# A stack of four conditioned blocks on one core: who writes the masked copies of the transposed keys in the two 16-head attention stages

## What is computed

```python
h = modulate(rmsnorm(x, norm1_w), sh_msa, sc_msa)
q, k, v = split(h @ qkv_w.T)                # 16 heads of 16
q, k = rmsnorm(q, q_norm_w), rmsnorm(k, k_norm_w)
q, k = rope3d(q, k, positions)
attn = softmax(einsum('bnhd,bmhd->bhnm', q, k) * 16 ** -0.5)
o = einsum('bhnm,bmhd->bnhd', attn, v) @ proj_w.T + proj_b
x = x + g_msa * o
```

## Time and profile before

| what | us |
| --- | --- |
| median of the runs (lowest, highest) | 2176.62 (2170.26, 2176.9) |
| the profiled execution | 2174.85 |
| its span (first to last instruction) | 2173.0 |
| PE, DVE, ACT, POOL busy in the span | 1923.1, 1320.1, 998.8, 817.1 |
| stage 1 without its ends (879 to 1190) | 311 |
| stage 2 without its ends (1510 to 1725) | 215 |

### The profile page before, as it was taken

One profiled execution on the slowest core, in us unless ns is written; L12 is line 12 of the kernel. 1 busy time (PEld: TensorE's weight loads), 2 busy tenths in 40 slices (PEclk: granted clock), 3 DMA queues, 4 the chain that ended last, 5 costly groups with the idle time before them and its releaser, 6 DMA issues. The chain is left out here.

```text
span 2173.0 us, 44682 instructions
## 1 busy us (share of the span) xinstructions
PE 1923.1 (89%) x17318; PEld 1488.1 (68%) x17318; DVE 1320.1 (61%) x2026; ACT 998.8 (46%) x1693; POOL 817.1 (38%) x733
## 2 busy tenths in 40 slices
PE   5999999999979997678887899969999889988897
PEld 3678777877867775466666677747676667776674
DVE  3454555455545554688878566757888745544554
ACT  2434433443346664456656333324555556653232
POOL 1210211021113434667777233456777633340000
PEclk7999999999999999899989999999999999999998
DMA  5100000000020000000000000010000000003222
GB/s 178 69 2 2 2 2 2 2 2 2 2 64 1 0 0 18 27 2 3 2 1 2 27 0 0 0 40 2 2 0 2 1 30 0 0 1 117 76 68 78
DMA packets 25884, 44.97 MB, mean 21 GB/s; under 512 B 3952, under 2 KB 11952, under 8 KB 25584
## 3 DMA queue, kind: packets, MB, share of 16 engines
q1 hardware_dynamic: 25712, 42.48, 5.9%
HBM read 36.18 MB, written 6.29 MB: 20 GB/s over the span
## 5 line engine op out<-in xcount | busy, mean ns | idle before, releaser
L1165 DVE TENSOR_TENSOR Glb<-Gfb,Ghb 128x512 fp32r<-128x512 f32 x176 | 164.3, 943 | 101.3 <-ACT Ghb L1116 99.6
L321 POOL TENSOR_TENSOR Tm<-Dv,MOD 128x512 f32<-128x512 f32 x96 | 110.5, 1171 | 248.7 <-DVE Dv L378 159.9
L439 PE MATMUL bank<-HH,W1b 128*128 128x512 f32 x448 | 185.0, 413 | 13.6 <-PEq L1445 7.3
L439 PE MATMUL O<-Ghb,W2b 128*128 128x512 f32 x352 | 144.1, 409 | 49.5 <-DVE Glb L1165 47.8
L440 PE MATMUL bank<-HL,W1b 128*128 128x512 f32 x448 | 178.0, 397 | 0.0
L441 PE MATMUL bank<-HH,W1b 128*128 128x512 f32 x448 | 177.9, 397 | 0.0
L459 POOL TENSOR_TENSOR spare<-RT 128x1 f32<-128x1 f32 x32 | 6.5, 202 | 414.9 <-DVE RT L450 414.9
L310 POOL TENSOR_TENSOR XS<-Tm 128x512 f32<-128x512 f32 x48 | 68.0, 1416 | 221.2 <-ACT Tm L276 221.1
L441 PE MATMUL O<-Ghb,W2b 128*128 128x512 f32 x352 | 138.6, 394 | 0.0
L440 PE MATMUL O<-Glb,W2b 128*128 128x512 f32 x352 | 138.3, 393 | 0.0
L1596 ACT ACTIVATE PTa<-bank 128x512 f32<-128x512 f32 x128 | 69.8, 594 | 126.2 <-PE bank L1476 126.1
(11 more groups left out here) (255 smaller groups left out, 5215.0 us busy)
## 6 DMA issues: line engine op xcount, KB each, us to landing
w<-l_w_dram SPq DMA_DIRECT2D x33, 256.0 KB, 3.5
wm<-w_mods_dram SPq DMA_DIRECT2D x6, 768.0 KB, 6.1
X<-xT_dram SPq DMA_DIRECT2D x16, 256.0 KB, 6.7
out_dram<-XO SPq DMA_DIRECT2D x8, 512.0 KB, 2.7
W2b_f<-l_w_dram SPq DMA_DIRECT2D x11, 256.0 KB, 5.2
WQK_f<-l_wqk_dram SPq DMA_DIRECT2D x8, 256.0 KB, 8.8
W1b_0f<-l_w_dram SPq DMA_DIRECT2D x8, 256.0 KB, 3.6
WV<-l_wv_dram SPq DMA_DIRECT2D x1, 1024.0 KB, 10.5
```

The costliest lines, as they stand in the source:

```text
L321: nc.gpsimd.tensor_tensor(Tm[:, k].rearrange("p (b t) -> p b t", t=T), Dv[:, k].rearrange("p (b t) -> p b t", t=T), m, ALU.mult).then_inc( ...
L439: nc.tensor.matmul(out, w_lo_ap, x_hi, start=first, stop=False)
L1165: nc.vector.tensor_tensor(Gl[m % gb][:], gf, Gh[m % gb][:].bitcast(F32), ALU.subtract).then_inc(g_lo.h, 1)
```

## The change

All four masked copies are written by ACT, each by one instruction of the kind of L1582; the last one counts `ka_sb`. The DVE instruction, its function and its semaphore's waits are gone. Nothing else moves.

```diff
@@ pe: weights_t
-  pe.wait_ge(ka_sb.h, ka_sb.at(tt + 2)); pe.wait_ge(kd_sb.h, kd_sb.at(tt + 2))
+  pe.wait_ge(ka_sb.h, ka_sb.at(tt + 2))
@@ pe: step, before the scores
-  pe.wait_ge(ka_sb.h, ka_sb.at(tt + 1)); pe.wait_ge(kd_sb.h, kd_sb.at(tt + 1))
+  pe.wait_ge(ka_sb.h, ka_sb.at(tt + 1))
@@ act: q_t
-  nc.scalar.activation(kb[:, :, 2], src, ACT.Copy, scale=hmask4[:, 2:3])
-  nc.scalar.activation(kb[:, :, 3], src, ACT.Copy, scale=hmask4[:, 3:4]).then_inc(ka_sb.h, 1)
+  for h in range(4):
+      last = nc.scalar.activation(kb[:, :, h], src, ACT.Copy, scale=hmask4[:, h:h + 1])
+  last.then_inc(ka_sb.h, 1)
@@ dve
-  def spread_k(tt, t):
-      dve.wait_ge(ka_sb.h, ka_sb.at(tt + 1))
-      dve.wait_ge(s_ready.h, s_ready.at(tt - 1))
-      src = TR_T4[:, 2 * P:4 * P].rearrange("p (gb k) -> p gb k", k=T)
-      nc.vector.tensor_tensor(KB[t % 2][:].rearrange("p g b h k -> p (g b) h k")[:, :, 0:2], src.unsqueeze(2).to_broadcast([P, 4, 2, T]),
-                              hmask4[:, 0:2].unsqueeze(1).unsqueeze(3).to_broadcast([P, 4, 2, T]), ALU.mult).then_inc(kd_sb.h, 1)
@@ dve: step
-  if ahead(t, more, tail, 1):
-      spread_k(tt + 1, (t + 1) % TL)
@@ dve: lead-in
-  spread_k(0, 0)
@@ end of stage
-  ka_sb.passed(NT); kd_sb.passed(NT)
+  ka_sb.passed(NT)
```

## The result

The changed kernel took 2191.64 us (median of 7 runs, 2183.33 to 2192.87) beside 2175.24 us (7 runs, 2162.93 to 2176.9) for the kernel before on the same chip: ratio 1.0075, 95% interval 1.0058 to 1.0093, so +16.4 us. The forecast was 2189.5 (+14.6), within 2180 to 2199. The profiled execution took 2192.87 us around a span of 2191.1.

A forecast was written before the change was run, and what follows sets the result against it. It took as bound the uncovered chain behind ScalarE's root at t = 3, once a chunk, and TensorE in other steps. Terms 9.9 + 2.9 + 0.7 + 1.4 - 2.0 + 1.7 = +14.6 on 2174.85 gave 2189.5 us, range 2180 to 2199.

The forecast's parts named there:

- (a): Two more ScalarE copies delay the root at t = 3 by 0.71 us in 14 chunks of both stages: +9.9 us.
- L370's wait: Sign: VectorE's norm waits for ScalarE's root about 2.1 us in stage 1 (from 0.75), 1.6 in stage 2 (from 0.18).
- (b): Every step's output copy comes 0.71 us later and delays TensorE's projection: +2.1 us in stage 2, +0.8 in stage 1.
- (e): The removed VectorE instruction saves 1.4 us in the two lead-ins and 0.6 at late scores in stage 1: -2.0 us.
- (f): Longer TensorE idle time before stage 2's mean makes its clock fall in one more chunk: +1.7 us, bounds 0 and 9.9.
- (c): At the loop's end in stage 1 the later output copy delays the next projection, once: +0.7 us.
- (d): In the last steps, at 1184.70 and 1723.62, the projection waits 0.71 us longer for the output copy: +1.4 us.
- the clean terms: All terms of the sum but the TensorE clock's, over both stages: +12.9 us.
- VectorE the bound: Rival: in the tails, removing VectorE's instruction gives back 0.68 us in each of 14, -9.5, so 2165.3 us; chance 0.07.
- ScalarE's idle time takes it: Rival: slack behind ScalarE's root absorbs its delay, leaving about +3 us, 2178; chance 0.15.
- The clock falls in each chunk: Rival: TensorE's clock falls before the mean in all six chunks of stage 2, +9.9 for +1.7, 2197.7 us; chance 0.18.
- ScalarE's busy time: Sign: over the whole kernel ScalarE's busy time goes up by about 60 us.

The follow-up runs named there:

- experiment 2: Kernel before, with ScalarE writing all four key copies only at t = 3 and VectorE's instruction kept in the other steps: 2187.2 us, 1.009.
- experiment 9: Changed kernel with ScalarE's root of the norm moved ahead of the exponential at t = 3: 2172.88 us, 1.0019.
- experiment 11: Changed kernel with POOL's L1417 in the tails of stage 2 held until HL is done: 2181.23 us, 1.0052.
- experiment 1: Kernel before with VectorE's key instruction left out and ScalarE keeping its two copies: 2176.09 us, 1.0033.
- the filled pair: Kernel before and changed kernel, both with matmuls of no use in TensorE's idle time at t = 1 of both stages: 2170.35 and 2187.04 us.
- the filling: Matmuls of no use at t = 1, eight in stage 1, six in stage 2; with VectorE's key instruction left out of the kernel before: 2172.43 us, 1.0016.
- experiment 4: Changed kernel with six matmuls of no use in TensorE's idle time before the mean of stage 2: 2184.41 us, 1.0071.

## Why the prediction was right, and where it was off

**(a), the root 0.71 later at t = 3: right.** Its price (0.355 a copy) and its place both hold: experiments 2 and 9 show that the step at t = 3 carries the change and that moving the root gives most of it back. With (b) at 0.25, experiment 11's 0.97 leaves 0.72 for it in stage 2. In stage 1 it can't be read apart. L370's wait came out under the forecast (1.35 and 1.59 instead of 1.6 and 2.1), because VectorE isn't earlier by all of its 0.69: with the VectorE instruction alone removed the wait grew by 0.44 in stage 2 and 0.12 in stage 1 (experiment 1), and 0.18 + 0.71 + 0.44 = 1.33, 0.75 + 0.71 + 0.12 = 1.58.

**(b), the output copy: right in stage 2**, 0.25 a chunk for a forecast 0.28. In stage 1 the filled pair gives (a) to (e) together as 6.2 for 5.9; the unfilled profiles show only 3.9. There the kernel before lost about 2 us to a TensorE at half clock (granted 0.53 from 1130 to 1140), which the changed kernel did not: its projection at 1135.09 takes 2.08 us, the changed one's at 1138.96 takes 1.16. The changed kernel in turn lost 3.7 in its first distance, where its clock was 0.64 for 0.95. (f) prices the clock in stage 2 alone; that such stretches move about in stage 1 was left out of the sum.

**(c)** was not isolated. **(d), the last steps: right.** The waits of the earlier trace rows, 0.16 and 0.20, are 0.89 and 0.93 in the changed kernel, 0.73 more each for a forecast 0.71. The second projection also takes 2.08 us, where it took 1.16:

```profile
1189.54 1.16 PE L1511 MATMUL O<-OSa,WOa 128*128 128x128 f32 x8 [0.89 <-ACT OSa L1574]
...
1743.87 2.08 PE L1511 MATMUL O<-OSa,WOa 128*128 128x128 f32 x8 [0.93 <-ACT OSa L1574]
```

**(e), the removed instruction, -2.0: not seen.** Taken away alone it made the kernel 0.33% slower, and 0.16% with the filling. The part of the argument that says VectorE only idles longer is shown. The 0.7 at the lead-ins (-1.4) was lost to the contest in stage 1: L370 starts 0.6 us sooner after the first subtraction (1.70 for 2.30) but takes 1.41 instead of 0.80, since POOL's L1415 has then only just begun, and HL starts 12.55 us after that subtraction for 12.53. In stage 2 it is 12.46 for 12.45 in this pair, and 12.22 for 12.92 in the filled one, so it shows there in one pair of two. The 0.6 of the late scores was overrated: with the keys early they wait for VectorE's subtraction instead, 0.58 us at 1182.99 for 0.70 at 1179.44.

**(f), TensorE's clock, +1.7: mis-sized, and the step behind it was incomplete.** I reckoned the idle time before the mean at 1.6 to 2.0 us. That is right where HL is short (1.57 after; 1.39 to 1.77 in experiment 11), and there nothing fell. I had not seen that HL and POOL's L1417 meet, although the rows of HL and POOL side by side in the kernel before show it: HL at 1.80 and 1.81 in two chunks, and even the rows that the forecast shows have HL at 1.23 in stage 2 and 1.53 in stage 1. After the change it is long in five of six, the idle time is then 1.97 to 2.36 us, and four of the seven means fell, to between 2.48 and 3.64 us; the seventh of them had fallen before too, so three are new where one was forecast. What this brought is 6.0 us in the distances, 6.2 in the window (experiment 11) and 4.5 in the medians (16.4 - 11.9), of which the window puts 3.6 down to the falls (experiment 4), in place of 1.7. The 6.2 and 4.5 include the two HLs that were long before. It lies inside the bounds of 0 to 9.9.

**The sum came out right partly by cancellation.** Against 14.6 stand 16.4: the contest and the clock gave about 3 to 4 more than allowed for, and the clean terms came out at 11.9 for 12.9, or 13.1 if the 1.2 us that experiment 11 gained on the two old long HLs is put back. Inside the clean terms (e) brought nothing like its -2.0, and which of the others was smaller by as much isn't shown.

**The rivals.** *VectorE the bound* fell with experiment 1. The forecast's case against it had HL idle for HH in nearly every tail; in stage 2 it was four of seven before (1.2 us in 4), and all seven after. *ScalarE's idle time takes it* fell with the 1.35 and 1.59 us waits and with experiment 9. *The clock falls in each chunk* came true in three of the six chunks, but filled on both sides the change costs the same 16.7 us, so that clock is no cause by itself.

ScalarE's busy time rose by 45 us, not 60, with 128 more instructions: in a row the busy times overlap, and each adds the 0.355 from start to start. I had counted durations of 0.47 there.

**Open:** what shifts POOL's start against HL's by the 0.01 us that decide the contest in chunks 2 to 4, when both hang on the same H; why the clock of stage 1 fell where it did; and (c).

## What to carry to other kernels

Before moving work to the engine that is half idle, look for its place in the serial chain: two copies of 0.355 us in one step of four cost about as much as the whole change (1.009 for 1.0075), though that engine was idle half of the time, and the same copies in the other three steps together came to 1.0037. Where VectorE and GpSimd instructions with SBUF operands meet, the one that starts second waits; where they start within some 0.02 us of each other, price both outcomes of the contest, and add them to the idle time of whoever waits behind, since that can bring TensorE's clock down too. If a late ScalarE step must stay, try its order first: putting the root ahead of the exponential gave back 12 us of 16.

## What the runs showed of the hardware

- In this kernel VectorE instructions with two SBUF inputs and POOL's that read SBUF hold each other up for most of an instruction: HL 1.23 or 1.81 us, POOL's first half 1.78 or 0.72, the norm 0.69 or 1.43. The time stands in the duration of the one that waits, not as idle time. The order of the starts decides, with 0.01 us in POOL's favour: POOL won in 41 of 41 tails of stage 2 in which it started at most 0.011 us behind HL, HL in 22 of 22 in which POOL started 0.017 or more behind. The outcome was the same in the same chunks in both profiles of the kernel before.
- In the changed kernel TensorE's granted clock fell after 2.17, 2.28, 2.30 and 2.52 us without work, not after 2.36, 1.97 or 1.57, and in no mean of experiment 11 after up to 1.77. In experiment 1 one mean fell after 1.90 us (2.75) and another after 1.90 didn't (1.98); in experiment 2 one didn't after 2.51. So the idle time just ahead isn't all that decides.
- A fall costs between 0.5 and 1.7 us in the mean itself, and some chunks lose more behind it (chunk 2 of the table: 1.85 over 35.21, of which HL and the mean explain 1.08).
